# Sixteen heads of queries in one transfer, with the planner's constants set anew, in a chain of transformer layers on one core

## The reference

```
x = L0(x, cond, ctx)    # modulated layer norm, self attention 0 (rope, mask), cross attention 1, MLP 0
x = L1(x, cond, ctx)    # attention over ctx, router, 3 experts, gate
x = L2(x, ctx, cond)    # cross attention 2
x = L3(x, cond, ctx)    # self attention 3, cross attention 4, MLP 1

def _attn(q, k, v, mask):
    s = jnp.einsum('bqhd,bkhd->bhqk', q, k) * scale
    s = jnp.where(mask, s, jnp.finfo(s.dtype).min)
    a = jax.nn.softmax(s, axis=-1)
    return jnp.einsum('bhqk,bkhd->bqhd', a, v)
```

## Time and profile before

| | |
|---|---|
| median of the runs | 981.49 us (980.85 to 984.12, 3 runs) |
| the profiled execution: its own time | 981.84 us |
| its span, first to last instruction | 980.0 us |
| PE, DVE, ACT, POOL busy | 94%, 72%, 57%, 15% of the span |
| mean granted clock of TensorE | 0.97 |
| DMA: mean rate, packets | 59 GB/s, 66323 |
| chain that ended last | PE 84%, DVE 6%, ACT 3%, issue 3%, DMA 2%, SP's queue 1% |

### The profile page before, as it was taken

The page is one execution under the profiler, slowest core; times in us unless marked ns, Lnnn a source line. Parts: engine busy times, 40 slices in busy tenths (PEclk is TensorE's granted clock), DMA queues, the critical chain, the costliest instruction groups (busy, mean ns, idle before and its releaser), DMA issues.

```text
span 980.0 us, 15448 instructions
## 1 busy us (share of the span) xinstructions
PE 919.4 (94%) x4986; PEld 397.1 (41%) x4986; DVE 707.8 (72%) x1933; ACT 559.4 (57%) x1036; POOL 145.1 (15%) x388
## 2 busy tenths in 40 slices
PE   3958999999999999999999999998999999999998
PEld 3622434433434444454444443333334333334443
DVE  5688898788888857552454556797988899886742
ACT  5023555664655667674437362574667677676673
POOL 1013000302011121110111120001212111022210
PEclk9777999999999999999999998998999999999999
DMA  8040320222011121100202033012032204014201
GB/s 310 33 129 2 85 61 26 67 77 74 16 55 50 58 78 35 34 7 1 65 4 63 7 115 85 7 65 67 23 115 76 65 2 123 15 34 105 68 14 33
DMA packets 66323, 57.49 MB, mean 59 GB/s; under 512 B 19407, under 2 KB 63427, under 8 KB 65988
## 3 DMA queue, kind: packets, MB, share of 16 engines
q1 hardware_dynamic: 64996, 54.73, 19.5%
q10 hardware_dynamic: 1248, 1.77, 0.5%
HBM read 31.01 MB, written 24.49 MB: 57 GB/s over the span
## 4 chain that ended last, share of the span: by engine, by line
PE 84%; DVE 6%; ACT 3%; issue 3%; DMA 2%; SPq 1%; POOL 0%; ACTq 0%; DVEq 0%; POOLq 0%
PE pv_bank L1540 16%; PE bank L1495 12%; PE bank L1518 11%; PE bank L1520 6%; PE bank L1522 4%; PE bank L1599 3%; PE bank L1646 3%; PE bank L1633 3%; PE bank L1651 3%; PE bank L1600 3%; PE bank L1498 2%; PE bank L1506 2%; PE bank L1565 2%; PE bank L1548 2%; PE bank L1468 2%
## 5 line engine op out<-in xcount | busy, mean ns | idle before, releaser
L1019 ACT ACTIVATE pr<-bank 128x512 f32<-128x512 f32 (+1 forms) x704 | 378.5, 598 | 194.8 <-PE bank L1520 103.0
L1271 DVE CUSTOM_DVE_ANT_0 bank<-bank,mask_q 128x512 f32<-128x512 f32 x256 | 171.3, 709 | 25.6 <-PE bank L1495 24.1
L1495 PE MATMUL bank<-ks,qs 97*128 97x512 bf16 x512 | 178.1, 391 | 12.2 <-issue 6.6
L1274 DVE TENSOR_REDUCE mx<-bank 128x1 f32<-128x512 f32 x256 | 163.4, 683 | 31.5 <-PE bank L1495 30.4
L1518 PE MATMUL bank<-qs,ks 103*128 103x512 bf16 x512 | 181.3, 385 | 1.3 <-DVE mx L1271 0.5
L1540 PE MATMUL pv_bank<-pr,va 128*32 128x512 f32 x1024 | 137.5, 608 | 1.1 <-ACT pr L1019 1.1
L1276 DVE TENSOR_REDUCE mx<-bank 128x4 f32<-128x308 f32 x192 | 83.7, 470 | 26.0 <-PE bank L1498 24.6
L1495 PEld LDWEIGHTS bank<-ks,qs 97*128 97x128 bf16 x512 | 43.9, 98 | 135.1 <-ACT pr L1019 28.1
L1520 PE MATMUL bank<-mask_k,identb 128*128 128x512 bf16 x256 | 98.1, 383 | 0.0
L915 POOL CAST mp<-mx 128x16 bf16<-128x16 f32 x80 | 16.0, 200 | 511.0 <-DVE mx L1271 203.0
L1518 PEld LDWEIGHTS bank<-qs,ks 103*128 103x128 bf16 x512 | 49.6, 98 | 71.8 <-ACT pr L1019 8.9
(11 more groups left out here) (219 smaller groups left out, 1197.6 us busy)
## 6 DMA issues: line engine op xcount, KB each, us to landing
qs<-q_parts SPq DMA_DIRECT2D x40, 384.0 KB, 4.6
q_parts<-xn SPq DMA_DIRECT2D x20, 384.0 KB, 2.6
ks<-k_parts SPq DMA_DIRECT2D x64, 96.0 KB, 3.7
q_parts<-xn SPq DMA_DIRECT2D x20, 256.0 KB, 2.2
k_parts<-u SPq DMA_DIRECT2D x8, 384.0 KB, 2.4
q_parts<-u SPq DMA_DIRECT2D x20, 128.0 KB, 2.1
qs<-mrow SPq DMA_DIRECT2D x160, 6.0 KB
late<-late_w SPq DMA_DIRECT2D x1, 2432.0 KB, 13.6
```

Source lines behind the costliest of these rows:

```text
L1019: act.activation(pr[0:K, 4 * (group % NSLOT) + t % 4, :], bank(k)[0:K, :], ACT.Exp, scale=SCALE).then_inc(act_done, 1)
L1271: dve.tensor_tensor_reduce(b[:, :], b[:, :], mask_q[:, qb, :], 1.0, -3e38, ALU.add, ALU.max, dst[:, qb, g, e:e + 1]).then_inc(dve_done, 1)
L1274: dve.tensor_reduce(dst[:, qb, g, e:e + 1], b[:, :], AX.X, ALU.max).then_inc(dve_done, 1)
L1495: ins = pe.matmul(b[:, :], qs[s][0:R, g, qb * P:(qb + 1) * P], ks[s][0:R, e, g, :], start=True, stop=True)
```

## The change

The second transfer of the queries is dropped: `stack` with `w = 0` moves all eight groups (768 KB) at once, with one semaphore per sample. PE waits for it ahead of the very first `max` tile of an attention, and not again at quarter 2. The planner's list of steps has one step fewer per attention (20 in all), its landing time for the queries is 5.2, and all its weights have new values, so the order of the steps of all lanes is made anew.

```
 def stack_queries(s, a):
-    return of(s, ("stack", a, 0, 0), ("stack", a, 0, 1))
+    return of(s, ("stack", a, 0, 0))

-LANDED = {... "stack": ((4.3, 4.6), (3.,) * HG), ...}
+LANDED = {... "stack": ((5.2,), (3.,) * HG), ...}
-TABLE_LOAD, TABLE_KEPT = 1.3, -130.721
+TABLE_LOAD, TABLE_KEPT = 1.3, -140.8847
-EAGER = {"chain": 0.4005, "rows": 0.2561, "max": 0.1002, "exp": 0.0224, "pv": -0.1116, "tables": 0.2095}
-URGE = ((0.635, 0.099, -0.344, -0.066, 0.264, 0.027, -0.328, -2.376),
-        (0.276, -0.005, 0.402, -0.008, 0.043, -0.252, -1.471, -2.1),
-        (0.516, -0.105, 0.134, -0.258, -0.122, -0.513, -0.978, -2.158),
-        (0.083, -0.07, 0.727, -0.128, -0.447, -0.731, -1.578, -1.504))
+EAGER = {"chain": 0.399842, "rows": 0.07979, "max": 0.100574, "exp": -0.075016, "pv": -0.100405, "tables": 0.270009}
+URGE = ((0.74012, 0.03783, -0.27802, -0.15316, 0.41701, 0.04614, -0.54898, -2.08212),
+        (0.32875, -0.01389, 0.77457, -0.02658, -0.00534, -0.33188, -1.18179, -1.54597),
+        (0.49358, -0.13414, 0.24272, -0.4084, -0.12269, -0.57189, -1.00619, -1.19114),
+        (0.05923, -0.03808, 0.15983, -0.11814, -0.46467, -0.77928, -1.49466, -0.93838))
-FAIR, CAP = 0.00245, 63.2916
+FAIR, CAP = 0.0024463, 69.10498

         if kind == "max":
-            first = [me("sp", "stack", a, 0, hg // 2)] + ...
+            first = [me("sp", "stack", a, 0, 0)] + ...

-        qread = [[sem(f"q_stacked{s}_{h}") for h in range(2)] for s in range(B)]; ...
+        qread = [sem(f"q_stacked{s}") for s in range(B)]; ...

-                        sp.dma_start(qs[s][0:STACK, 4 * part:4 * part + 4, :], v[:, 4 * part:4 * part + 4]).then_inc(qread[s][part], 16)
+                        sp.dma_start(qs[s][0:STACK, :, :], v).then_inc(qread[s], 16)

                 def max(k, s, a, hg, t):
-                    if t == 0 and hg % 2 == 0:
-                        pe.wait_ge(qread[s][hg // 2], 16 * (a + 1))
                     if (hg, t) == (0, 0):
+                        pe.wait_ge(qread[s], 16 * (a + 1))
```

More of the change, by code:

```diff
@@ L221 @@
 TILE_HOLDS = {"max": (.135, .385), "exp": (.22, .49)}
-LANDED = {"load": 2.5, "store": 2.2, "part1_out": 2.4, "parts_out": 2.4, "stack": ((4.3, 4.6), (3.,) * HG), "ctx_out": 2.7, "ctx_stack": 2.5, "max_rows": 1.9}
+LANDED = {"load": 2.5, "store": 2.2, "part1_out": 2.4, "parts_out": 2.4, "stack": ((5.2,), (3.,) * HG), "ctx_out": 2.7, "ctx_stack": 2.5, "max_rows": 1.9}
 LOADED = {"w_ada": 0., "w_mod": 3., "trig": 4., "mask": 6., "setup": 9., "late": 13.}
@@ L265, in before @@
             a, hg, t = rest
-            first = [me("sp", "stack", a, 0, hg // 2)] + ([me("sp", "stack", a, 1, hg)] if a in SELF else [me("sp", "ctx_stack", CL[a])] + ([me("pool", "bias", 2)] if a == 2 else []))
+            first = [me("sp", "stack", a, 0, 0)] + ([me("sp", "stack", a, 1, hg)] if a in SELF else [me("sp", "ctx_stack", CL[a])] + ([me("pool", "bias", 2)] if a == 2 else []))
             second = []
@@ L706, in build @@
         qwrit = [sem(f"q_parts_written{s}") for s in range(B)]; kwrit = [sem(f"k_parts_written{s}") for s in range(B)]
-        qread = [[sem(f"q_stacked{s}_{h}") for h in range(2)] for s in range(B)]; kread = [[sem(f"k_stacked{s}_{hg}") for hg in range(HG)] for s in range(B)]
+        qread = [sem(f"q_stacked{s}") for s in range(B)]; kread = [[sem(f"k_stacked{s}_{hg}") for hg in range(HG)] for s in range(B)]
         mrows = [[sem(f"max_rows{s}_{hg}") for hg in range(HG)] for s in range(B)]
```

## The result

The changed kernel takes 998.02 us (median of 4 runs, 996.15 to 1000.35) beside 981.38 us for the kernel before in the same runs: a ratio of 1.0172, 95% interval 1.0149 to 1.0195. It is slower by about 17 us. The forecast was 979, within 972 to 987.

A forecast was written before the change was run, and what follows sets the result against it. PE was taken as the bound, busy 919.4 of 980.0 us. The terms summed as 981.84 - 0 - 2.7 + 0 = 979.1 us for the profiled execution, 978.8 against the median, stated as 979.0; range 972 to 987.

The forecast's parts named there:

- What bounds the kernel: PE, busy 919.4 of 980.0 us; from 400 us on, three to five us idle in each 100.
- Step 1, SP's issues: SP's queue: twenty DMA issues of about 0.48 us leave; earlier keys could give 0 to 1.0 us; taken as 0.
- The transfer's landing: One 768 KB transfer of queries lands 4.9 us after issue in quiet places, about 6 in full ones; bounds 3.5 and 7.0.
- Steps 2 and 3, the longer wait: First max tile waits for all sixteen heads: 0 in eight self attentions, 0 in twelve cross attentions, upper end there 16.8 us.
- the cover of 1.1 us: First self attention: queries land at about 61.4, the second transfer of keys at 62.5, so the longer wait is hidden.
- rival B: Slower: whole transfer becomes a wait in cross attentions behind 400 us, half exposed by 1.2 us each; 986 us; chance 0.26.
- Step 4, the new order: Planner puts first self attention tiles 0.9 us later at 590.41, 669.80, 763.76; other lanes' work fills it; gain 2.7 us.
- the term for everything else: Changed weights move steps all over the list; taken as 0, bounds 6.1 us of waits gone or as many new ones.
- Rival A: Waits near 590, 670 and 764 go altogether, 6.1 us filled, and the clock follows; 974 us; chance 0.22.
- Rival C: Whole change: transfer no shorter than two, new order neither better nor worse; time stays at 981.5 us; chance 0.10.
- What would show it: Checks of issues, landing and waits; wrong if PE's idle time between 100 and 980 changes more than the named places account for.

The follow-up runs named there:

- the exchanged weights: Two runs, planner making new lists: changed kernel with the old weights, 1041.91 us, 1.0615; kernel before with the changed kernel's weights, 1076.77 us, 1.0967.
- the new middle: Old order with one transfer, but steps 43 to 1300 in the changed kernel's order: 995.36 us, ratio 1.0121 to the kernel before.
- the new end: Old order with one transfer, but steps from 1301 on in the changed kernel's order: 990.09 us, ratio 1.0086 to the kernel before.

## Why the prediction was wrong, point by point

**What bounds the kernel** was read rightly: PE, with idle time after 400 us. What those rows could not say, and the exchanged weights showed, is that 6% idle is the merit of one particular order.

**Step 1, SP's issues**: right, 20 issues fewer save nothing that shows.

**The transfer's landing** failed in size. I took 4.9 us in quiet and about 6 in full places, because the same bytes land then as two halves; it takes 5.5 to 5.9 in quiet and 6.1 to 7.1 in full places, 5.9 as the median of 20. The 4.9 was also the quickest of the twenty places of the kernel before, where the median for both halves is 5.4. The Trainium skill's figures in "DMA: Bandwidth & Descriptors" (6.15 us for 1 MB in section Bandwidth, and about 2.0 us fixed in section Anatomy of one DMA, both for transfers issued by GpSimd, where here SP issues) gave an estimate of 6.6; the usual 5.6 of the quiet places lies between, 0.7 us above the one and 1.0 below the other. The sentence that a trace with these bytes in flight must give the time of one transfer left out that two issues also bring the engines up sooner.

**Steps 2 and 3, the longer wait**: taken as 0, it and the later landing make 2.4 to 4.0 us in the old order (1.0024 with two transfers, 1.0041 with one). In the self attentions the cover of 1.1 us went in part with the later landing; the changed kernel's first tile at 65.14 names the queries, not the keys. In cross attentions rival B's mechanism is there, but once in the changed kernel (1.8 us at 399.51), not in four places of 1.2.

**Step 4, the new order** is the step that decided, and it failed twice. The gain of 2.7 us was argued from one constant, the due time of the first tile: the five waits ahead of line 1494 came to 12.0 us, not to 9.1 less 2.7. (By its own rows the planner was 1.6 to 2.6 us early there, 4.7 against 6.3, 6.6 and 7.3, not "2 us and more".) And the term for everything else was set at 0 with bounds of about 6 us, taken from the three large waits of the earlier trace rows. That bound was no bound. What a new order can cost is not what the old one's named waits hold; it is all the time that the old one avoids, and the runs put it at 1.35% here and near 6% and 10% for two other lists. The forecast, both rivals and the range (972 to 987) rest on that term, so all were too low.

**Rival A** is refuted: the wait of 2.66 us fell to 0.62 (676.05), but the others stayed or grew and one of 2.82 came new (834.05). **Rival B** had the right sign but, for the changed kernel, a mechanism that shows in one place only, and under a third of the size. **Rival C**, nothing changes, is refuted by the interval.

**What would show it**: the last sentence of the prediction named this outcome (idle time between 100 and 980 changed by more than those places hold, hence the new order elsewhere). It did not get a chance of its own.

## What to carry to other kernels

Where an order of all engines is written by a planner, its constants are part of the program: a diff that sets them anew replaces every engine's list, and the local edit beside them is the small part (0.4% of 1.7% here). Price the two apart, give the new list a term as wide as the idle time that the old one avoids, and test them crosswise: the old list with the new operation, the new list with the old one. Change nothing in such a planner without fitting the weights again, and rely on its own clock for differences of a per cent and more only. Read the granted clock beside PE's busy time before a longer busy time is put down to the order of steps alone.

## What the runs showed of the hardware that I had not expected

One transfer of 768 KB in rows of 1 KB lands 5.9 us after its issue as the median of twenty, where two of 384 KB issued 0.4 to 0.7 us apart are both there after 5.4, and four of 192 KB after 5.4 too. The first of the two is there after about 4 us and the first of the four after 2.8. Splitting a transfer that the first consumer needs only in part was worth its extra issues, by about 0.4% here.

The busy time of the same 4986 matmuls is not a constant either: 918.2 us in the old order with one transfer, 927.1 with the new middle (granted clock 0.963 against 0.971), 928.5 in the new order with two transfers (0.970). Idle time alone does not lengthen it, since with the new end PE idles for 6.1 us more than in the old order and is busy for only 1.5 more (919.7).
